# Two LoRA layers folded into one Strassen product chain: the first product's 16 tiles are written out of PSUM by ScalarE in place of VectorE

## The reference, cut to what matters

```python
def layer0(x, ids, W, bias, A, Bw):      # W is (out, in)
    h = einsum('bsd,brd->bsr', x, A[ids])
    return einsum('bsd,od->bso', x, W) + bias + einsum('bsr,bor->bso', h, Bw[ids])

def layer1(x, ids, W, b, As, Bs):
    h = einsum('bti,bir->btr', x, As[ids])
    return einsum('bti,oi->bto', x, W) + b + 2 * einsum('btr,bro->bto', h, Bs[ids])

x = x + layer0(x, ...)                    # x is (8, 512, 2048) fp32
x = x + layer1(x, ...)
```

## Time and profile before

| What | Value |
|---|---|
| Median of 3 runs | 2079.47 us (2079.36 to 2080.51) |
| Profiled execution, its own time | 2080.5 us |
| Its span in the profile | 2078.8 us |
| TensorE (PE) busy | 2063.9 us (99%), 9460 matmuls |
| VectorE (DVE) busy | 1595.9 us (77%), 2180 instructions |
| ScalarE (ACT) busy | 725.1 us (35%), 1291 instructions |
| GpSimd (POOL) busy | 724.5 us (35%), 513 instructions |

### The profile page before, as it was taken

One profiled execution on the slowest core, in us unless ns is written; L12 is line 12 of the kernel. 1 busy time (PEld: TensorE's weight loads), 2 busy tenths in 40 slices (PEclk: granted clock), 3 DMA queues, 4 the chain that ended last, 5 costly groups with the idle time before them and its releaser, 6 DMA issues.

```text
span 2078.8 us, 28061 instructions
## 1 busy us (share of the span) xinstructions
PE 2063.9 (99%) x9460; PEld 1717.2 (83%) x9460; DVE 1595.9 (77%) x2180; ACT 725.1 (35%) x1291; POOL 724.5 (35%) x513
## 2 busy tenths in 40 slices
PE   8999999999999999999999999999999999999999
PEld 7887788888888888888888888888888888888887
DVE  5688868977887787677878677877677886777885
ACT  5562323333333333333333333333333333333332
POOL 2135414551404552223544121545040445131453
PEclk9999999999999999999999999999999999999999
DMA  9996748995737795746796655798564789574776
GB/s 287 293 310 186 240 143 258 285 300 158 240 109 242 238 325 166 217 124 205 237 314 212 185 171 157 231 295 276 147 211 135 214 269 318 145 220 120 217 220 193
DMA packets 283899, 458.05 MB, mean 220 GB/s; under 512 B 27500, under 2 KB 88940, under 8 KB 283244
## 3 DMA queue, kind: packets, MB, share of 16 engines
q1 hardware_dynamic: 215788, 333.54, 52.3%
q10 hardware_dynamic: 67968, 122.71, 19.3%
HBM read 382.75 MB, written 74.45 MB: 220 GB/s over the span
## 4 chain that ended last, share of the span: by engine, by line
PE 90%; DVE 3%; issue 1%; DMA 1%; POOL 0%; SPq 0%; ACT 0%; DVEq 0%; POOLq 0%; ACTq 0%
PE acc L1575 28%; PE acc L1581 28%; PE acc L1586 28%; PE h_acc L1496 2%; PE h_acc L1492 2%; PE acc L1506 1%; DVE w_lo L1083 1%; PE h_acc L1495 1%; DVE xop_lo L1109 0%; DVE vp_lo L1078 0%; DMA x_pre<-w_t 0%; DMA w_raw<-v_t 0%; DVE c_acc L1191 0%; DVE x_sum L1098 0%; DVE x_pre L1211 0%
## 5 line engine op out<-in xcount | busy, mean ns | idle before, releaser
L893 POOL TENSOR_TENSOR w_raw<-w_raw,w_second 128x512 f32<-128x512 f32 x464 | 661.1, 1426 | 1212.8 <-DMA w_second<-wc_t 688.1
L1083 DVE TENSOR_TENSOR w_lo<-w_raw,w_hi 128x512 fp32r<-128x512 f32 x672 | 587.2, 876 | 414.6 <-ACT w_hi L930 412.3
L930 ACT ACTIVATE w_hi<-w_raw 128x512 fp32r<-128x512 f32 x672 | 424.3, 632 | 1234.1 <-PE acc L1586 1046.9
L1575 PE MATMUL acc<-xop_hi,w_hi 128*128 128x512 f32 x2688 | 726.0, 391 | 3.1 <-DVE c_pre L1261 1.8
L1581 PE MATMUL acc<-xop_lo,w_hi 128*128 128x512 f32 x2688 | 723.3, 390 | 0.0
L1586 PE MATMUL acc<-xop_hi,w_lo 128*128 128x512 f32 x2688 | 722.1, 390 | 0.0
L1575 PEld LDWEIGHTS acc<-xop_hi,w_hi 128*128 128x128 f32 x2688 | 502.6, 188 | 107.4 <-ACT w_hi L930 4.7
L1586 PEld LDWEIGHTS acc<-xop_hi,w_lo 128*128 128x128 f32 x2688 | 503.8, 188 | 104.2
L1581 PEld LDWEIGHTS acc<-xop_lo,w_hi 128*128 128x128 f32 x2688 | 504.0, 188 | 103.6
L1109 DVE TENSOR_TENSOR xop_lo<-x_sum,xop_hi 128x512 fp32r<-128x512 f32 x240 | 158.7, 681 | 3.8 <-ACT xop_hi L943 3.0
L1098 DVE TENSOR_TENSOR x_sum<-x_in 128x512 f32<-128x512 f32 x160 | 158.5, 991 | 0.7
(11 more groups left out here) (107 smaller groups left out, 1027.9 us busy)
## 6 DMA issues: line engine op xcount, KB each, us to landing
w_raw<-wc_t SPq DMA_DIRECT2D x448, 256.0 KB, 3.7
w_second<-wc_t ACTq DMA_DIRECT2D x320, 256.0 KB, 4.3
w_raw<-v_t SPq DMA_DIRECT2D x208, 256.0 KB, 4.1
w_second<-v_t ACTq DMA_DIRECT2D x144, 256.0 KB, 4.6
x_in<-x_t SPq DMA_DIRECT2D x128, 256.0 KB, 6.0
out_t<-c_out SPq DMA_DIRECT2D x128, 256.0 KB, 5.3
w_part<-w_t SPq DMA_DIRECT2D x32, 512.0 KB, 8.2
x_pre<-w_t SPq DMA_DIRECT2D x64, 256.0 KB, 6.1
```

What stands on the lines that cost most here:

```text
L893: nc.gpsimd.tensor_tensor(w_raw[:, r, :], w_raw[:, r, :], w_second[:, n % RAW2, :], ALU.add if sign > 0 else ALU.subtract).then_inc(w_summ ...
L930: nc.scalar.activation(flat(w_hi[:, s % RING, :, :]), w_raw[:, r, :], ACT.Copy).then_inc(w_hi_ready, 1)
L1083: nc.vector.tensor_tensor(flat(w_lo[:, s % RING, :, :]), w_raw[:, s % RAW, :], f(flat(w_hi[:, s % RING, :, :])), ALU.subtract).then_inc(w_ ...
L1575: nc.tensor.matmul(bank[:, :], w_hi[:, s % RING, kk, :], xop_hi[:, place, :], start=(k == 0), stop=False)
```

## The change

The 16 instructions of L1240 leave VectorE. ScalarE gets a function `evict_first(m)` with two activations (Copy with scale -1 and +1), with the same waits. For m = 0 and 1 it stands at the end of ScalarE's slots 3 and 4; for m = 2 to 7 behind `w_hi` and ahead of the parts, in slots 7, 8, 11, 12, 15 and 16. TensorE's, GpSimd's and SyncE's programs are unchanged.

```diff
+            def evict_first(m):
+
+                act_e.wait_ge(step_done, finished(M5, m) + 1)
+                bank = shaped(0, bank_of(M5, m)[:, :])
+                if m == 0:
+                    act_e.wait_ge(t_filled, E_USE + 1)
+                if m == 2:
+                    act_e.wait_ge(t_filled, T_USES)
+                if m == 4:
+                    act_e.wait_ge(small_stored, 3 * 16)
+                for blk, sign in PRODUCTS[M5][5]:
+                    nc.scalar.activation(c_of(0, block_no(*blk), m), bank, ACT.Copy, scale=float(sign)
+                                         ).then_inc(c_updated, 1)
...
                 load_second(g + 2 + RAW2)
+                for qq, m in evictions(g):
+                    if qq == M5 and m >= 2:
+                        evict_first(m)
                 for n in parts_split(g)[:1]:
                     split_part_hi(n)
...
                     a_split_hi(v)
+                for qq, m in evictions(g):
+                    if qq == M5 and m < 2:
+                        evict_first(m)
...
-                if q == M5 and m == 0:
-                    dve.wait_ge(t_filled, E_USE + 1)
-                if q == M5 and m == 2:
-                    dve.wait_ge(t_filled, T_USES)
-                if q == M5 and m == 4:
-                    dve.wait_ge(small_stored, 3 * 16)
...
-                    if q == M5:
-
-                        nc.vector.tensor_scalar(c, bank, float(sign), None, ALU.mult).then_inc(c_updated, 1)
-                        continue
...
-                for qq, m in evictions(g):
-                    if qq == M5 and m >= 2:
-                        evict(qq, m)
...
-                    if qq != M5 or m < 2:
+                    if qq != M5:
                         evict(qq, m)
```

## The result

In 22 runs of each on one chip the changed kernel took 2083.44 us in the median and the kernel before 2080.22: a ratio of 1.0014, 95% interval [1.0008, 1.0019]. It is slower by 1.7 to 4.0 us. The prediction was 2078.9 with a range of 2077.0 to 2081.6 and "no change" at 90%. By size this is within its 0.2%, but the kernel did not get 0.6 us faster; it got some 3 us slower, and the time is outside the range. Of the 4.5 us between forecast and measurement 0.75 lie in the kernel before itself, 2080.22 in these 22 runs for 2079.47 in the 3 that the forecast started from.

What follows compares the result with a forecast made beforehand. TensorE was taken as the bound, with only its pauses in the first 200 us open to change. +0.11 + 0.71 - 0.53 - 0.9 = -0.6 us, carried to the median of 2079.47, gave 2078.9 us, range 2077.0 to 2081.6.

Steps and rivals of the forecast that it cites:

- The step-5 pauses: TensorE near 67.85 and 71 us: first pause 0.11 us longer, a new second one of 0.71 behind ScalarE's pair.
- The pause at 135: TensorE's pause of 0.53 us before 135.15 goes as VectorE's second vp_lo ends earlier: -0.53 us.
- the prediction's count of four: Four TensorE pauses before 67.85, 135.15, 158.56 and 197.17, together 3.38 us, taken as all that can be won before 200 us.
- The pause at 158.56: TensorE's pause before step 17 goes because ScalarE does the pair for m = 7 earlier: -1.18 us there.
- rival 2: ScalarE becomes late: pairs finding no gap delay TensorE's turned parts; +1.7 us, 2081.2; chance 20%.
- the one at 169 us: VectorE's start on x_pre at 169.16 moves by about 0; TensorE keeps -0.9 us at 200 us.
- The bounds, 0 and -2.06: Limits set on what TensorE keeps at 200 us, around the worked value of -0.9 us.
- The pause near 197: TensorE's wait for VectorE before 197.17 was to grow from 0.88 to about 1.2 us.
- The chain of waits: From the pair at 157.13 through c_acc, w_lo and SyncE's last x_pre loads to VectorE's work from 169.16 on.
- VectorE is held up once less: GpSimd's eight additions from 167.22 start 1.18 us earlier, sparing VectorE up to 1.09 us from 169.16 on.
- Rival 3: GpSimd's move costs VectorE what the pair gave, its earlier start helps no one: +0.3 us, 2079.8; chance 26%.
- a transfer that now comes late for all: One of two ways to be over 0.2% slower, above 2083.6 us; 5% for both together.

Runs made afterwards that it cites:

- only_m1: The kernel before with only the pair of evictions for m = 1 moved to ScalarE; 2080.83 us, ratio 1.0001.
- before_delayed: The kernel before, SyncE holding step 16's w_raw load and the four x_pre loads behind it until VectorE has written c_out of m = 7; 2082.53 us, 1.0005.
- not1_first: The changed kernel with m = 1's pair left on VectorE and two groups of x_pre loads issued ahead of the w_raw loads; 2078.12 us, 0.9984.
- fill19: The changed kernel with eight more matmuls on TensorE ahead of step 19, no result changed; 2081.45 us, 1.0005.
- pool_waits: The changed kernel with GpSimd's addition for m = 7 held back until w_lo of step 18 is written; 2079.89 us, 1.0001.
- again_after: The changed kernel unaltered, run again for a second profile; 2082.71 us.
- only_m7: The kernel before with only the pair of evictions for m = 7 moved to ScalarE; 2083.81 us, 1.0019.
- before_delayed2: The kernel before, SyncE holding step 16's w_raw load and the first four x_pre loads behind it until GpSimd's addition for m = 7; 2085.12 us, 1.0017.

## Why the prediction was wrong

*Up to 160 us it holds.* The pair takes 1.07 us (1.06). The step-5 pauses cost +0.11 and +0.68 (+0.11 and +0.71), and only_m1 shows them alone. The pause at 135 is gone, and with it smaller ones, such as 0.11 before 132.92, which the prediction's count of four left out: TensorE gains 1.08 us from 73 to 136 us (0.53 foreseen). This gain is known roughly only, for the second execution of the kernel before loses 0.65 us to the first in the same stretch. The pause at 158.56 is gone; from 136 to 160 us TensorE gains 1.59 (1.18 foreseen). ScalarE's later pairs cost TensorE nothing, so rival 2 is out. Even the contention was seen: GpSimd's addition for m = 7 at 154.96 ("near 155.5"), `c_acc` at 1.78 ("about 1.8").

*The step that failed is the one at 169 us:* "Its start moves ... by about 0 if GpSimd's addition for m = 7 ... moves to 155.5 and holds up c_acc", and with it "-0.9 us as what TensorE keeps at 200 us". VectorE's start on `x_pre` moved by +0.77 and not by 0, and TensorE kept nothing: from 160 to 203 us it lost 3.45, so that from 136 to 203 us it stands at -1.59 + 3.45 = +1.86 where the prediction had -0.9. The bounds, 0 and -2.06, did not hold it either; at 203 us against 60 it stood at +1.6. The pause near 197, which should have grown from 0.88 to about 1.2, is 0.60; the price was paid ahead of it, in a pause of 1.80 that was foreseen nowhere. The sum of the steps as measured is +0.79 - 2.67 + 3.45 = +1.57 us, against a ratio that says +1.7 to +4.0. What lies between is not explained by these traces.

Three errors lie in that step.

1. *The chain's last load was taken for the burst.* The chain of waits names the load issued at 162.80 and 6.26 us behind it. I moved only that end. But ten loads of 256 KB were on their way together; and VectorE had the last tile 11.4 to 12.6 us behind the first issue in every kernel of the table, but from 5.9 to 8.4 us behind the last. In before_delayed the last load is where it was, and the tile came 0.9 late. The first load hangs on `w_lo` of step 18, and this on the `c_acc` that I had at 1.8 us myself. I weighed the 1.0 us lost there against the 1.28 that the pair gives back and called the difference about 0. But the pair stood *behind* this `w_lo`, at 157.13: its going helps the second group of loads alone, and the first pays in full.

2. *An absolute time was used against a moving partner.* The pauses go and TensorE, with GpSimd's `a_twice` and `c_out` additions that it releases, runs 2.1 us ahead. The landing does not. So `x_pre` was 2.9 us late where it counts.

3. *The sign of GpSimd's head start.* "VectorE is held up once less" was the opposite of what happened. VectorE's additions and GpSimd's take turns from about 171 to 187 us. In the kernel before, first GpSimd's eight additions, then three of VectorE's beside them:

```profile
178.02 13.84 POOL L884 TENSOR_TENSOR c_out<-c_out,x_pre 128x512 f32<-128x512 f32 x8
```

```profile
178.53 1.77 DVE L1109 TENSOR_TENSOR xop_lo<-x_pre,xop_hi 128x512 fp32r<-128x512 f32 x1
180.23 1.78 DVE L1191 SCALAR_TENSOR_TENSOR c_acc<-x_pre,bias,c_acc 128x512 f32<-128x512 f32 x1
...
183.63 1.77 DVE L1109 TENSOR_TENSOR xop_lo<-x_pre,xop_hi 128x512 fp32r<-128x512 f32 x1
```

A turn is 180.23 - 178.53 = 1.70 us. Whoever starts late loses places in that order. How many can be read from VectorE's first eviction behind the chain, here of the kernel before and, below it, of the changed one:

```profile
185.33 0.68 DVE L1261 TENSOR_TENSOR c_out<-acc,c_out 128x512 f32<-128x512 f32 x1
```

```profile
185.99 0.68 DVE L1271 TENSOR_TENSOR c_out<-acc,c_out 128x512 f32<-128x512 f32 x1
```

Counted from the start of GpSimd's eight `c_out` additions it starts at 185.33 - 178.02 = 7.31 us in the kernel before and at 185.99 - 175.28 = 10.71 in the changed one: 3.40 later, which is two turns. The distance is 7.30 or 7.31 in all five kernels of the table where `x_pre` is up to 1.5 us late, and 10.71 to 10.73 in all five where it is 2.2 late or more; between 1.5 and 2.2 no run decides. It also goes the other way: in not1_first, where `x_pre` is 0.7 us early against TensorE, it is 5.60, one turn less. Against TensorE the two turns are 2.6 to 2.8 us, since GpSimd's additions themselves begin 0.6 to 0.8 earlier. In four of the five late kernels the `w_lo` behind this eviction then meets one more addition of GpSimd (1.79 at 187.19, for 0.68) and some 0.7 more is lost, which makes the 3.3 to 3.5 of the table; in fill19 it takes 0.68, and the table has 2.8.

The Trainium skill (SBUF — State Buffer, "SBUF: two separate sides") calls the shared ports an exclusive lock and "not a bandwidth split": whoever starts first has it for the whole instruction. The trace agrees for the single instruction, 0.68 alone and 1.77 beside GpSimd. I used that rule for what one addition costs and not for what it makes of two queues: a place in the order, which a start a little too late loses in whole turns. That places are lost in whole turns is measured; that this comes from the lock is inferred from it: no run took GpSimd's additions away from 170 to 187 us.

Rival 3 ("the end gives nothing back", 2079.8) had the right direction and a tenth of the size, +0.3 for some +2.9 by the ratio. Rival 2 (+1.7) came nearer by its number alone; its cause, a pair on ScalarE that finds no gap, did not occur behind step 5. That the change could make things *worse* than losing the gain, through a transfer, stood only in the 5% of "a transfer that now comes late for all".

## What to carry to other kernels

When the chain of waits ends in a transfer, look how many were issued with it: the ten loads here landed by the first issue and not by the last, so the first issue's releaser is what to guard. When a change lets one engine run ahead, ask of every transfer that does not run ahead with it how late it is *against that engine*, and whether its consumer shares turns with another: there the price was a step and not a slope. An instruction that is freed to start earlier (here GpSimd's) may need a wait of its own, as pool_waits shows; the better version tried is the change without m = 1, with the loads moved ahead, 0.9984 [0.9975, 0.9993].

## What the runs showed of the hardware that I had not expected

- A pause of 1.80 us before 187.41 was followed in one execution by 3.4 us at the lower of the clock's two levels, 1.2 GHz (0.57 granted over 187 to 191 us, four matmuls in 1.93 us). Pauses of 1.69, 1.79 and 1.72 us at the same place in again_after, only_m7 and before_delayed2 were not; the row of only_m7 for the same four microseconds has 1.00:

```profile
187.00:191.00 4.00, 3.28 (x16) 2.67 (x16) 4.00 (x5) 0.00 (x0) 1.75 (x2) 1.00 0.29 85
```

- It cost 0.2 us at most there: the changed kernel lost 3.45 us from 160 to 203 us, again_after 3.27 and only_m7 3.41, since VectorE and not TensorE set the pace.
- A delay of 0.9 to 1.5 us of a tile that starts a chain of additions in turns was absorbed to 0.2 us; one of 2.2 cost 3.3. VectorE's distance from GpSimd behind the chain takes steps of one turn of 1.70 us: 5.60 in not1_first, 7.31 in before, and 10.71, two steps further, in the changed kernel.
